# One-core macaron kernel: half-block front, next rows' transposes at unit 12, row statistics at units 0 and 1

## The reference, cut to what matters

```python
def _route(x_flat, router_w, bias):
    scores = sigmoid(x_flat @ router_w.T)            # 16 experts, 4 groups
    ...                                              # top 2 groups, top 4 experts, weights normed, times 2.5
def _L0_ffn_ref(x, ...):
    combine = (one_hot(topk_idx, E) * tw[..., None]).sum(1)
    h = einsum('td,edf->etf', x, gate_w); u = einsum('td,edf->etf', x, up_w)
    y = einsum('etf,efd->etd', silu(h) * u, down_w)  # all 16 experts for all tokens
    routed = einsum('etd,te->td', y, combine)
    return routed + (silu(x @ sh_gate_w) * (x @ sh_up_w)) @ sh_down_w
x = L0_attn_x                                        # (4, 1024, 128) float32
x = x + 0.5 * ffn(layernorm(x))
x = x + attention(layernorm(x))                      # 32 heads of 4, no softmax, group norm
x = x + 0.5 * ffn(layernorm(x))
```

## Time and profile before

| | us |
|---|---|
| median of 3 runs (lowest to highest) | 665.79 (665.75 to 666.4) |
| the profiled execution, its own time | 665.98 |
| its span, first to last instruction | 664.2 |
| PE busy | 658.0 (99%) |
| DVE, POOL, ACT busy | 519.2, 445.1, 406.4 |
| first product of a gate starts at | 10.25 |

### The profile page before, as it was taken

One profiled execution on the slowest core, in us unless ns is written; L12 is line 12 of the kernel. 1 busy time (PEld: TensorE's weight loads), 2 busy tenths in 40 slices (PEclk: granted clock), 3 DMA queues, 4 the chain that ended last, 5 costly groups with the idle time before them and its releaser, 6 DMA issues.

```text
span 664.2 us, 10555 instructions
## 1 busy us (share of the span) xinstructions
PE 658.0 (99%) x3169; PEld 550.7 (83%) x3169; DVE 519.2 (78%) x1441; ACT 406.4 (61%) x817; POOL 445.1 (67%) x385
## 2 busy tenths in 40 slices
PE   8999999999999999999999999999999999999997
PEld 7888888888888888888888888888888888888886
DVE  6896969698785977869778788787785968868664
ACT  5876575656666566666567655676566565655554
POOL 6997666666756678565775667766667666666663
PEclk9999999999999999999999999999999999999999
DMA  9816060603307033070240700604207042250700
GB/s 232 276 51 256 5 252 1 242 14 109 148 0 256 1 120 136 1 255 1 88 168 1 245 12 22 249 1 175 97 20 254 0 162 111 60 212 3 270 0 33
DMA packets 30262, 75.38 MB, mean 113 GB/s; under 512 B 3569, under 2 KB 12545, under 8 KB 30209
## 3 DMA queue, kind: packets, MB, share of 16 engines
q1 hardware_dynamic: 30208, 74.74, 31.9%
HBM read 72.11 MB, written 2.62 MB: 113 GB/s over the span
## 4 chain that ended last, share of the span: by engine, by line
PE 98%; DVE 1%; issue 0%; ACT 0%; POOL 0%; DVEq 0%; POOLq 0%
PE gateP L449 10%; PE yP L453 10%; PE yP L449 10%; PE yP L450 10%; PE upP L449 10%; PE gateP L453 10%; PE upP L453 10%; PE gateP L450 10%; PE upP L450 10%; PE prepP L490 2%; PE attP L507 1%; PE prepP L482 1%; PE backP L471 1%; PE yP L578 1%; PE backP L563 1%; PE attP L563 1%
## 5 line engine op out<-in xcount | busy, mean ns | idle before, releaser
L340 POOL TENSOR_TENSOR A_lo<-A,A_hi 128x512 fp32r<-128x512 f32 x287 | 370.1, 1291 | 203.4 <-ACT A_hi L817 203.4
L843 ACT ACTIVATE gateP<-gateP 128x512 f32<-128x512 f32 x252 | 146.6, 582 | 201.9 <-PE gateP L453 201.0
L1160 DVE TENSOR_TENSOR T<-gateP,CB 128x512 f32<-128x512 f32 x252 | 173.2, 687 | 88.5 <-ACT gateP L843 80.7
L817 ACT CAST A_hi<-A 128x512 fp32r<-128x512 f32 x287 | 176.0, 613 | 11.3 <-DVE A L1191 7.8
L1191 DVE TENSOR_TENSOR A<-upP,T 128x512 f32<-128x512 f32 x254 | 175.6, 691 | 8.7
L449 PE MATMUL gateP<-XT_hi,W_hi 128*128 128x512 f32 x288 | 118.6, 412 | 0.0
L449 PE MATMUL yP<-A_hi,W_hi 128*128 128x512 f32 x288 | 112.6, 391 | 0.0
L453 PE MATMUL yP<-A_lo,W_hi 128*128 128x512 f32 x288 | 112.5, 391 | 0.0
L453 PE MATMUL gateP<-XT_lo,W_hi 128*128 128x512 f32 x288 | 112.5, 391 | 0.0
L450 PE MATMUL gateP<-XT_hi,W_lo 128*128 128x512 f32 x288 | 112.3, 390 | 0.0
L450 PE MATMUL yP<-A_hi,W_lo 128*128 128x512 f32 x288 | 112.1, 389 | 0.0
(11 more groups left out here) (231 smaller groups left out, 645.2 us busy)
## 6 DMA issues: line engine op xcount, KB each, us to landing
CB<-combT SPq DMA_DIRECT2D x126, 512.0 KB, 6.9
out_dram<-X SPq DMA_DIRECT2D x7, 256.0 KB, 2.0
X<-in_L_attn_x_dram SPq DMA_DIRECT2D x3, 512.0 KB, 9.4
W_in<-in_L_ffn_gate_w_dram SPq DMA_DIRECT2D x4, 256.0 KB, 5.1
W_in<-in_L_ffn_up_w_dram SPq DMA_DIRECT2D x4, 256.0 KB, 5.1
W_in<-in_L_ffn_down_w_dram SPq DMA_DIRECT2D x4, 256.0 KB, 5.5
X<-in_L_attn_x_dram SPq DMA_DIRECT2D x2, 256.0 KB, 3.1
combT<-CT SPq DMA_DIRECT2D x16, 32.0 KB, 1.8
```

Source lines behind the costliest of these rows:

```text
L340: pool.tensor_tensor(A_lo[:, slot, :], A[:, slot, :], A_hi[:, slot, :].bitcast(F32), ALU.subtract).then_inc(low_done, 1)
L817: act.copy(A_hi[:, v % SLOTS, :], A[:, v % SLOTS, :]).then_inc(high_done, 1)
L843: act.activation(dst, gateP[u % 2][:, :], ACT.Silu).then_inc(silu_done, 1)
L1160: dve.tensor_tensor(T[:, u % TS, :], silu, weights, ALU.mult).then_inc(gate_weighted, 1)
```

## The change

It does eight things:

1. R_in and ebias are loaded through ACT's queue, ahead of ACT's first instruction, not through SP's between the halves of X.
2. `WARM` goes from 13 to 9, and the two filler products behind `transpose_next(0)` are gone.
3. Statistics are merged by BN_AGGR, one per tile, and one or two small operations, in place of the seven of `merge_stats` and the PSUM variants; `parts` is gone.
4. The first block's chain goes in halves of 256 columns: XN, two transposes to each of two banks, copy to XT, XT_hi, XT_lo (first half on DVE, second on POOL between W_lo of unit 0 and unit 1).
5. `first_units` starts with the four passes of unit 0 that don't need XT_lo; gate(5) stands ahead of the routing weights; `transpose_weights(0)` ahead of `spread(0)`, and `spread(1)` behind up(4).
6. POOL does `step_rstd(1)` behind W_lo of unit 5, and W_lo of units 8 and 9 at its units 2 and 3.
7. In all later steps `rows` stands at w 0, `aggregate` and `stats` at w 1, `step_rstd` at w 3, `normalise` at w 9 (four tiles at once), `transpose_next` at w 12 behind `transpose_weights`, `next_full` at w 13.
8. The combined weights go through a quarter of `attP`, with waits in the attention's stages at u 9, 14 and 33, and at w 12 PE waits for ACT's fourth attention operation and not its second.

The diff, cut to its core:

```diff
-    WARM, FILL = 13, 2
+    WARM, FILL = 9, 2
+            return prepP[:, 0:P] if isinstance(t, int) and t == 0 else attP[:, 3 * P:4 * P]   # combine_bank
...
             sp.dma_start(X[:, 0:TILES, :], x_v[0][:, 0:TILES, :]).then_inc(x_first, 16)
-            sp.dma_start(R_in[:, :], router_w).then_inc(router_in, 16)
-            sp.dma_start(ebias[:, :], bias.unsqueeze(0).broadcast_to([P, E])).then_inc(ebias_in, 16)
...
-            SPLIT_AT = {4: 10, 5: 11, 7: 12, 8: 13, 9: 14, 10: 15, 11: 16, 12: 17}
+            SPLIT_AT = {2: 8, 3: 9, 4: 10, 5: 11, 7: 12, 8: 13, 9: 14, 10: 15, 11: 16, 12: 17}
-                    if w == 14 and not last:
+                    if w == (14 if early else 3) and not last:
                         step_rstd(2 * p + s + 2)
...
-            for unit in range(SHARED):
-                split_low(unit)
             pool.wait_ge(xn_ready, 2)
+            split_low(0)
+            pool.wait_ge(xt_hi_ready, 1)
+            cols = HALVES[1]
+            pool.tensor_tensor(XT_lo[:, 0, cols], XT[:, cols], XT_hi[:, 0, cols].bitcast(F32),
+                               ALU.subtract).then_inc(xt_lo_ready, 1)
+            for unit in range(1, 6):
+                split_low(unit)
             step_rstd(1)
-            for unit in range(SHARED, 10):
+            for unit in range(6, 8):
                 split_low(unit)
...
-                elif not (isinstance(t, int) and t in (0, 2)):
-                    pe.wait_ge(ct_ready, t)
+                else:
+                    pe.wait_ge(route_seq, ROUTE_OPS * t)          # transpose_next
...
-                gate(0)
-                up(0)
+                pe.wait_ge(w_lo_done, 1)
+                pe.wait_ge(xt_hi_ready, 1)
+                for i, dst in enumerate((gateP[0], first_up[0])):
+                    pe.matmul(dst[:, :], W_hi[:, 0, i, :], XT_hi[:, 0, :], start=True, stop=False)
+                    pe.matmul(dst[:, :], W_lo[:, 0, i, :], XT_hi[:, 0, :], start=False, stop=False)
+                pe.wait_ge(xt_lo_half, 1)
+                pe.wait_ge(xt_lo_ready, 1)
...
                 gate(4)
-                pe.wait_ge(route_seq, ROUTE_OPS)
+                gate(5)
+                transpose_weights(0)
                 spread(0)
+                pe.wait_ge(mul_done, 1)
+                up(4)
+                pe.wait_ge(ct_ready, 1)
                 spread(1)
-                transpose_weights(0)
-                gate(5)
...
-                            pe.wait_ge(att_act, ATT_ACT * (p - ATT0) + (5 if s else 2))
+                            pe.wait_ge(att_act, ATT_ACT * (p - ATT0) + (5 if s else 4))
-                    if w == 17 and not last:
+                    if w == (17 if early else 12) and not last:
                         transpose_next(t0 + s + 2)
...
-                    if w in (15, 16) and not last:
-                        normalise(t0 + s + 2, 2 * ((p + 1) % BATCH) + s, w - 15)
+                    if w == 13 and not early and not last:
+                        next_full(t0 + s + 2)
+                    if w in ((15, 16) if early else (9,)) and not last:
+                        for part in (w - 15,) if early else (0, 1):
+                            normalise(t0 + s + 2, 2 * ((p + 1) % BATCH) + s, part)
...
+            act.dma_start(R_in[:, :], router_w).then_inc(router_in, 16)
+            act.dma_start(ebias[:, :], bias.unsqueeze(0).broadcast_to([P, E])).then_inc(ebias_in, 16)
...
+            def aggregate(t, dst):
+                dve.wait_ge(stats_seq, 4 * t + 1)
+                for j in range(TILES):
+                    ins = dve.bn_aggr(dst[:, j, :], bst[:, j, :])
+                ins.then_inc(stats_seq, 1)
             def stats(t):
-                merge_stats(stats_seq, 4 * t, bst, nmean[:, :], vareps[:, :], parts)
+                dve.wait_ge(stats_seq, 4 * t + 2)
+                dve.tensor_scalar(nmean[:, :], mv[:, :, 0], -1.0, None, ALU.mult)
+                dve.tensor_scalar(vareps[:, :], mv[:, :, 1], EPS, None, ALU.add).then_inc(stats_seq, 2)
-                    if w == (12 if early else 11) and not last:
+                    if w == (12 if early else 0) and not last:
...
+            for cols, bank, made, done in zip(HALVES, (prepP, backP), (xt_half, xt_done),
+                                              (xt_copied_half, xt_ready)):
+                dve.wait_ge(made, 1)
+                dve.tensor_copy(XT[:, cols], bank[:, HALVES[0]]).then_inc(done, 1)
+                if bank is prepP:
+                    stats(1)
```

More of the change, by code:

```diff
@@ L485, in logits @@
             def logits(t):
-                pe.wait_ge(xt_ready, t + 1)
-                bank = backP if isinstance(t, int) and t < 2 else prepP
+                if isinstance(t, int) and t == 0:
+                    pe.wait_ge(xt_copied_half, 1)
+                else:
+                    pe.wait_ge(xt_ready, t + 1)
+                bank = logits_bank(t)
                 for j in range(TILES):
+                    if isinstance(t, int) and t == 0 and j == TILES // 2:
+                        pe.wait_ge(xt_ready, 1)
                     mm = pe.matmul(bank[:, j * E:(j + 1) * E], XT[:, j * P:(j + 1) * P], RT[:, :],
@@ L495, in transpose_weights @@
                 pe.wait_ge(route_seq, ROUTE_OPS * (t + 1))
[L496 to L498 removed]
+                pe.transpose(combine_bank(t), comb[:, :], ident[:, :]).then_inc(ct_done, 1)
             def attention_stage(u, b):
@@ L595, in up @@
                     one(first_up[u], u, 1).then_inc(up_done, 1)
-                gate(0)
-                up(0)
+                pe.wait_ge(w_lo_done, 1)
[5 more added lines that the diff above has]
+                pe.wait_ge(xt_lo_ready, 1)
+                for i, (dst, done) in enumerate(((gateP[0], gate_done), (first_up[0], up_done))):
+                    pe.matmul(dst[:, :], W_hi[:, 0, i, :], XT_lo[:, 0, :], start=False,
+                              stop=True).then_inc(done, 1)
                 gate(1)
@@ L681, in pair @@
                         if w == 12 and not early:
+                            if attention and s == 1:
+                                attention_stage(u, p - ATT0)
+                            if first:
+                                pe.wait_ge(setup_sb, 4)
                             transpose_weights(t0 + s + 1)
-                    if w == 17 and not last:
+                    if w == (17 if early else 12) and not last:
                         transpose_next(t0 + s + 2)
-                    if attention:
+                    if attention and u != 30:
                         attention_stage(u, p - ATT0)
@@ L693, in _ @@
             keep_busy(FILL)
-            transpose_next(0)
-            keep_busy(FILL)
+            for h, (bank, done) in enumerate(((prepP, xt_half), (backP, xt_done))):
+                pe.wait_ge(xn_ready, h + 1)
+                for j in range(TILES // 2):
+                    mm = pe.transpose(bank[:, j * P:(j + 1) * P], XN[:, h * TILES // 2 + j, :], ident[:, :])
+                mm.then_inc(done, 1)
             pe.wait_ge(setup_sb, 1)
@@ L865, in pair @@
                     if not (last and s >= 1):
-                        if w == (6 if early else 0):
-                            next_full(t0 + s + 1)
+                        if first and u in (6, UNITS):
+                            next_full(s + 1)
                         if w == (6 if early else 1):
@@ L886, in _ @@
                 split_high(unit)
-            next_high(0, 0)
+            for cols, copied, done in zip(HALVES, (xt_copied_half, xt_ready), (xt_hi_half, xt_hi_ready)):
+                act.wait_ge(copied, 1)
+                act.copy(XT_hi[:, 0, cols], XT[:, cols]).then_inc(done, 1)
             route_silu(0)
@@ L1211, in pair @@
                         rows(t0 + s + 2, 2 * ((p + 1) % BATCH) + s)
-                    if w == (13 if early else 12) and not last:
-                        if early:
-                            stats_in_psum(2, prepP[:, FREE_AT:FREE_AT + 4 * TILES], 2)
-                        else:
-                            stats(t0 + s + 2)
+                    if w == (13 if early else 1) and not last:
+                        aggregate(t0 + s + 2, mv)
+                        stats(t0 + s + 2)
                     if first and u == PAIR - 1:
```

95 lines of the change are left out of this document (26 added, 69 removed).

## The result

The kernel after takes **667.84 us** (median of 18 runs, 666.53 to 669.0), the kernel before 665.84 on the same chip (18 runs, 665.68 to 666.47). The ratio is **1.0027**, 95% interval 1.002 to 1.0035: slower by 2 us, where I had forecast 0.8 less, and outside my range.

The account below looks back on a forecast made before the run. PE was taken to bound the middle and POOL's queue the front; -0.6 (front) - 0.25 (merged groups) = -0.85 against the profiled 665.98 gave 665.1, with the median 0.19 lower 665.0 us; range 664.2 to 666.4.

Parts of the forecast that it names:

- DVE's own margin in units 16 and 17 of step 0: First step: DVE's margin of 0.5 us holds, as its queue gets shorter by some 0.4 us.
- The middle costs nothing: Later steps: moved work fits idle time; tightest in attention pairs, 0.42 + 0.25 us of DVE work in 1.56 idle.
- the sum stands: Front: PE's clock is up by 7.9 us at the latest, so 8 fewer warming records cost nothing.
- rival B: Front: clock still down at 9.1 us, first passes 0.43 apart, first Silu late, +0.7 - 0.25, 666.3 us; chance 0.12.
- by the rule it may come late: Front: the clock needs sustained activity, transposes don't count, so full clock may come late; the case of rival B.
- the front's 0.6: Front: with POOL's queue as bound, PE starts the pass of 26.56 at 25.97, 0.6 us sooner.
- POOL's sum: Front: POOL's work from the end of XT_lo (9.7) through the fourth A_lo sums to 16.2 us, ending at 25.9.
- merging the groups: PE, small transposes moved beside other small products in 13 places: saves 0.03 us in each of 9, 0.25 us net.
- BN_AGGR at 0.10: DVE's statistics merge: one BN_AGGR takes 0.10 us, with 0.22 as the upper bound.
- rival C: DVE: BN_AGGR is long, 0.5 us, delaying the front and four attention pairs, some 669.4 us; chance 0.06.
- XN at 6.45: Front, DVE: statistics and merges end and XN can start at 6.45 us, against 6.55 before.
- rival A: Front: POOL is no bound and ACT's rounding is next, -1.1 - 0.25, 664.4 us; chance 0.2.

Follow-up runs that it names:

- e5_psum13: As e2_fill, but the merge in unit 13 of step 0 is again that of the kernel before (operands in PSUM, no BN_AGGR): 665.53 us, ratio 0.9992.
- e2_fill: The changed kernel with two more filler products behind the router's transpose and two between the halves of the first logits: 666.42 us, ratio 1.0008.
- e1_stt: The changed kernel with its two small merge operations, nmean and vareps, written as SCALAR_TENSOR_TENSOR instead of TENSOR_SCALAR: 666.44 us, ratio 1.0014.
- e4_before_warm9: The kernel before with WARM 9 in place of 13 and without the two fillers behind the first transposes: 667.95 us, ratio 1.0021.
- e6_front: As e5_psum13, with block 1's two small operations in the front placed behind both copies of the transposes instead of between them: 665.34 us, ratio 0.9989.
- e8_unit17: As e6_front, with the next rows' transposes at unit 17 and their copy at unit 0 again, in all steps: 666.15 us, ratio 1.0001.
- e7_lo_dve: As e6_front, but DVE makes both halves of XT_lo and POOL none: 665.50 us, ratio 0.9989.

## Why the prediction was wrong, and where it was right

**Wrong, in the first step: "DVE's own margin in units 16 and 17 of step 0 is 0.5 us, but its queue ... gets shorter by some 0.4 us ..., so that it holds."** This is the step that failed in the profiled pair. I priced the two small operations at 0.20 to 0.25 us together from the earlier trace rows; `nmean` alone took 1.75. The queue became 1.2 us longer and not 0.4 shorter, PE stood 0.6 for `T`, and +1.1 us stayed (e5_psum13: 1.1 back in the trace, 0.9 in the median). What I overlooked was not the size but a resource: which operands lie in SBUF while POOL works. The text of before, which keeps one operand in PSUM here, and L906's 350 ns, gave it away. "The middle costs nothing" held; nowhere in steps 1 to 15 does PE wait, because at w 0 and 1 the same `nmean` at 0.7 us fits into DVE's idle time. In pair 2 the time from 171.23 to 172.32 us was filled, 1.1 us of the 1.56 and not 0.67.

**Wrong, in the median: "By the trace, where it was up by 7.9 at the latest, the sum stands".** The sum put the 8 fewer warming records and the missing fillers at nothing. With four more products of ones the median is 666.42 and not 667.84 (e2_fill), so 1.4 us hang on them, and they carry it from the edge of my range to well outside. The mechanism (too little warming, passes 0.43 apart) was named with its signs as rival B, but at 0.12 and 666.3. By the mean clock it came in 12 of 18 runs. Against my forecast it was to cost 1.3 us; the levels are 1.1 and 2.3 above the best. So the price of the lower one was near, which is partly luck, since no execution of that level was profiled, and that of the other was not: I had let the clock be late for the first Silu alone, and in e1_stt's profile it is down from 8.73 to 15.55, after having been up. Some 13 passes at 0.43 in place of 0.227 are 2.6 us, which no lead of 1 us ahead of POOL absorbs. The Trainium skill, TensorE: Matmul & The Clock Gate, Part 1 and Part 4, has the throttle released by sustained activity, at a moment that varies, with transposes not counting as such. The runs agree on the varying moment (5.31 in the trace of e1_stt, 14.5 in that of e4_before_warm9); that the transposes are what failed to count, none of them shows apart from the holes between them. Where "by the trace, the sum stands" and "by the rule it may come late" stood side by side I trusted one execution of the kernel before, with 13 products and not 9.

**Wrong in size: the front's 0.6.** POOL's sum was right: from the end of XT_lo, 10.26, to 25.20 + 1.31 = 26.51 are 16.25 us, forecast 16.2 (one term, the reciprocal root with its shift, is 1.29 by the rows and not 1.35; the sum hardly feels it). Its start was not: 10.26 and not 9.7, since `nmean` (0.74) stood ahead of the second copy. That is again the same mechanism. Half of it was worth having back: 0.24 us by e6_front, where the landing of the weights takes over. Beyond, 0.13 was lost between the fourth and the fifth `down`, since a PE that resumes behind a wait starts its second pass 0.34 or 0.35 later and not 0.227 (24.34 to 24.68).

**Wrong in size: merging the groups.** I had 0.25; it is 0.63 in the pair of profiles (1.21 to 0.58), 0.67 in e8_unit17 against e6_front, and 0.49 in e6_front against before. Outside the attention it saves 0.033 each, as forecast (1.207, 1.174, 1.141 in steps 1 to 3). In the attention's pairs, for which I had put 0.03 a pair (one merge of two saving nothing), a pair saves 0.09 to 0.14. Passes behind a group stand 0.23 to 0.235 apart for some ten of them, which the distance of two passes in the earlier trace rows doesn't hold; this may be a part, but it was not taken apart further.

**Right.** BN_AGGR at 0.10 (0.38 / 4 = 0.095), so rival C was out; XN at 6.45 (6.44); POOL as the bound of the front, with PE's wait for A_lo (rival A out: POOL was the bound, its rows good to 0.05 us); the hole ahead of the first routing weights gone; no cost of the moved statistics in the middle. The sum as it came, in the pair of profiles: 0.0 for the front, +0.13 behind it, +1.08 at unit 16, -0.63 for the merges, 0.58 us, and 0.55 was measured; the median has 1.4 us of clock on top.

## What to carry to other kernels

Before replacing several small DVE instructions by fewer, look where their operands lie: with all of them in SBUF, each can stand until POOL's running work ends (all 15 `nmean` of after did), and this shows as a duration, not as a wait; read the min, median and max of such a line, and ask which row of POOL ends at the same time. Products that only keep the matrix engine busy ahead of its first real work are part of the timing, so whoever removes some must look at many runs and at the clock of each, not at one profile. And when one queue is the bound of the start, ask what its first element waits for, down to the DMA, before moving work off it.

## What the runs showed of the hardware

- A DVE TENSOR_SCALAR or SCALAR_TENSOR_TENSOR on 128x4 elements with all operands in SBUF took 0.68 to 1.76 us in after and e1_stt while POOL was at TENSOR_TENSOR from SBUF (0.40 in e7_lo_dve, where less of POOL's instruction was left), and 0.15 to 0.16 with an operand in PSUM beside the same POOL instructions, or with POOL idle. At unit 13 it outlasted the end of the first A_lo and stood through the second, which followed without a gap; in the 13 later steps it came free at the end of the first, though XT_lo followed as closely. Why it differs is open. BN_AGGR (0.36 for four), with one SBUF input, ran unhindered beside them.
- The clock can fall again: in e1_stt at full level from 5.31 us, at half from 8.73 to 15.55, with PE busy for 2.59 of the 3.20 us from 5.4, on transposes and small products. Where four more products of ones filled that stretch, no run of 22 had a mean clock below 0.999.
- The runs of one kernel stood on three levels some 1.1 us apart (666.6, 667.7, 668.9), each with its own mean granted clock (0.999, 0.997, 0.995).
- BN_AGGR costs 0.095 us for 6 numbers in and 2 out per partition, in a run of four.
